# Normalisation moved behind the projections, and a later second score step, in a fused attention and mixture-of-experts kernel

## The reference

```python
xn = (x - mean(x)) / sqrt(var(x) + 1e-5)                 # over the 128 channels
# attention, 16 heads of 8 channels, causal
q, k, v = split(xn @ w_attn)
scores = q @ k.T / sqrt(8) + causal - log1p(softplus(decay_raw) * log1p(i - j))
y = softmax(scores) @ v
attn = y @ w_proj
# feed-forward, 8 experts of 128 -> 512 -> 128, each token takes the best 2
logits = xn @ Wr.T
gate = softmax over the two largest logits
ffn = sum over the 2 experts of gate * (silu(xn @ W1.T) @ W2.T)
out = x + attn + ffn
```

## Time and profile before

| what | value |
|---|---|
| median of 3 runs | 531.16 us (529.22 to 532.96) |
| profiled execution, its own time | 531.62 us |
| its span, first to last instruction | 529.8 us |
| PE busy | 482.3 us, 91% |
| DVE, ACT, POOL busy | 68%, 63%, 64% |
| chain that ended last | 72% PE, 18% DVE, 3% POOL, 2% ACT |

### The profile page before, as it was taken

One profiled execution on the slowest core, in us unless ns is written; L12 is line 12 of the kernel. 1 busy time (PEld: TensorE's weight loads), 2 busy tenths in 40 slices (PEclk: granted clock), 3 DMA queues, 4 the chain that ended last, 5 costly groups with the idle time before them and its releaser, 6 DMA issues.

```text
span 529.8 us, 13373 instructions
## 1 busy us (share of the span) xinstructions
PE 482.3 (91%) x4316; PEld 351.6 (66%) x4316; DVE 360.5 (68%) x1406; ACT 335.6 (63%) x600; POOL 338.4 (64%) x566
## 2 busy tenths in 40 slices
PE   7767999989999999999999999999999999999920
PEld 6545566555565665665565565666999999999910
DVE  7595997988988878888878878872433333333326
ACT  3578878878878878878878878776232333333300
POOL 2873555556888878876878888970454555555524
PEclk9988999999999999999999999999999999999975
DMA  6566591570460451450460451355466677666449
GB/s 179 168 232 207 156 219 47 157 214 8 136 185 23 135 173 36 137 164 23 136 181 27 137 165 50 107 171 141 121 201 190 209 215 207 207 183 207 131 166 319
DMA packets 71826, 80.38 MB, mean 152 GB/s; under 512 B 8638, under 2 KB 52672, under 8 KB 71760
## 3 DMA queue, kind: packets, MB, share of 16 engines
q1 hardware_dynamic: 67440, 71.06, 45.8%
q0 software_dynamic: 4320, 8.47, 4.5%
HBM read 48.11 MB, written 31.84 MB: 151 GB/s over the span
## 4 chain that ended last, share of the span: by engine, by line
PE 72%; DVE 18%; POOL 3%; DMA 2%; ACT 2%; issue 2%; SPq 0%; DVEq 0%; ACTq 0%; POOLq 0%
PE psT L1291 22%; PE psO L1309 13%; PE ps L1336 12%; DVE scores L1121 12%; PE psT L1363 12%; PE ps L1266 7%; PE psM L1250 2%; POOL xn_all L734 2%; DVE x_all L535 2%; PE ps L1327 1%; PE psM L1320 1%; DMA probs<-picked_dram 1%; POOL rstd L727 1%; ACT probs L884 1%; DMA decay_in<-decay_raw 1%
## 5 line engine op out<-in xcount | busy, mean ns | idle before, releaser
L1121 DVE CUSTOM_DVE_ANT_0 scores<-ps,wdist 128x256 f32<-128x256 f32 (+3 forms) x512 | 218.6, 486 | 28.1 <-PE ps L1266 25.4
L765 POOL TENSOR_SCALAR scores<-scores,row_max 128x256 f32<-128x256 f32 (+2 forms) x384 | 177.5, 477 | 62.9 <-DVE row_max L1121 61.6
L884 ACT ACTIVATE probs<-psT 128x512 f32<-128x512 f32 x320 | 173.7, 594 | 54.8 <-PE psT L1291 54.4
L1291 PE MATMUL psT<-ident,scores 128*128 128x128 f32 x1280 | 177.2, 281 | 3.4 <-ACT probs L884 2.8
L1291 PEld LDWEIGHTS psT<-ident,scores 128*128 128x128 f32 x1280 | 137.6, 141 | 63.7 <-issue 37.5
L783 POOL DMA_INDIRECT picked_dram<-scores,row_ring x71 | 69.7, 982 | 80.6 <-DVE scores L1173 79.1
L893 ACT ACTIVATE scores<-ps 128x512 f32<-128x512 f32 x71 | 42.4, 597 | 95.1 <-PE ps L1336 95.1
L846 ACT ACTIVATE scores<-scores,row_max 128x512 f32<-128x512 f32 x128 | 84.8, 714 | 0.0
L1309 PE MATMUL psO<-probs,values 128*32 128x512 f32 (+3 forms) x1024 | 82.0, 438 | 0.0
L1336 PE MATMUL ps<-scores,wdist 128*128 128x128 f32 x568 | 75.3, 276 | 0.8 <-DVE scores L1161 0.8
L1363 PE MATMUL psT<-wdist,scores 128*128 x568 | 75.3, 276 | 0.6 <-ACT scores L893 0.6
(11 more groups left out here) (140 smaller groups left out, 277.4 us busy)
## 6 DMA issues: line engine op xcount, KB each, us to landing
wdist<-w1t SPq DMA_DIRECT2D x71, 256.0 KB, 3.2
k_rows<-k_dram SPq DMA_DIRECT2D x64, 96.0 KB, 2.8
q_rows<-q_dram SPq DMA_DIRECT2D x64, 96.0 KB, 2.6
row_ring<-rows_dram SPq DMA_DIRECT2D x71, 65.0 KB, 3.0
probs<-picked_dram SPq DMA_DIRECT2D x8, 512.0 KB, 6.8
rows_dram<-row_ring SPq DMA_DIRECT2D x7, 585.0 KB, 5.8
k_dram<-k_parts SPq DMA_DIRECT2D x7, 384.0 KB, 2.3
q_dram<-q_parts SPq DMA_DIRECT2D x7, 384.0 KB, 2.6
```

The costliest lines, as they stand in the source:

```text
L765: last = nc.gpsimd.tensor_scalar(part, part, -1.0, row_max[:, r, tile, quad:quad + 1], ALU.mult, ALU.add)
L884: nc.scalar.activation(probs[:, at.ring(2), w, :], psT[:, w % 2], ACT.Exp, scale=-1.0).then_inc(exp_ready, 1)
L1121: last = nc.vector.tensor_tensor_reduce(out=scores[:, r, u, col:col + n], in0=bank[:, col:col + n], in1=wdist[:, at.g * QUADS + quad, SEQ ...
L1291: last = nc.tensor.transpose(psT[:, w % 2, place * P:(place + 1) * P], scores[:, at.ring(2), u, col + key * P:col + (key + 1) * P], ident[:])
```

## The change

Four things change.

1. Rows of batches 1 to 7 are turned raw. The weights are centred instead: PE multiplies `w_qkv` (the router's weights are now its last 8 columns) by `centre` = identity - 1/128 (step WC), and ACT copies the result back over `w_qkv`; that takes the mean off. The factor 1/std comes later: on the keys and queries by a scaling of `xt` on DVE (XN) with factors that PE turns (RT), ACT copies, SP stores (RO) and loads back spread over the partitions (RB); on the values in step V, which becomes four activations with a factor per token; on the logits in LC, which becomes a multiplication on POOL. The normalised rows that the experts need are made by POOL in slots 3 to 8 (NR, five tiles a slot).
2. The order around the start: all XB and six of the eight VL stand ahead of slot 0, in banks of their own; 12 of the 16 LN now lie in slots 0, 1 and 2 (LN 8 to 11 in slot 1 and LN 12 to 15 in slot 2, between exponentials); POOL writes the second part of the queries (QP) and takes all ten units of the maximum's subtraction in slots 0 to 2, where ACT takes none.
3. P1(1) stands behind PV 0 and 1 from slot 1 on, on every engine.
4. The sends start one slot later (slot 9).

```diff
-FIRST_SEND_SLOT = 8
+FIRST_SEND_SLOT = 9
-EARLY = {0: (("VL", 12), ("LN", 4), ("LN", 5)),
...
+EARLY = {0: {1: (("VL", 24), ("LN", 4), ("LN", 5)),
+             2: (("VL", 28), ("LN", 6), ("LN", 7)) + tuple(("LC", b * GROUPS) for b in range(6)),
+             3: (("RT", 1), ("V0", 0), ("XN", 4), ("LC", 24), ("LC", 28), ("CZ", 1)),
+             4: tuple((kind, b * GROUPS) for kind, b in (("VS", 4), ("VS", 5), ("XS", 3), ("VS", 6), ("VS", 7), ("XS", 4))
+                      ) + (("RO", 1), ("XS", 20), ("XS", 24), ("XS", 28))},
+         1: {2: (("LN", 8), ("LN", 9)), 3: (("LN", 10), ("LN", 11), ("CZ", 2))},
+         2: {2: (("LN", 12), ("LN", 13)), 3: (("LN", 14), ("LN", 15), ("CZ", 3))}}
+FIRST_ROWS_SLOT, ROW_TILES = 3, 5
...
+GROUPS_BY_POOL = 3
...
+def act_units(c):
+
+    return ACT_UNITS if c >= GROUPS_BY_POOL else ()
...
+    per_batch("XT", -4)
+    per_batch("RB", -4)
     p1(0)
-    p1(1)
+    if n == 0:
+        p1(1)
     step("TE", n - 1, NGROUP, 0, 2)
...
     step("PV", n - 2, NGROUP, 0)
     step("PV", n - 2, NGROUP, 1)
+    if n > 0:
+        p1(1)
     per_batch("KR", -3)
...
     p1(4)
+    per_batch("XN", -4)
     step("TE", n - 1, NGROUP, 8, 10)
...
+    first = TILES + ROW_TILES * (n - FIRST_ROWS_SLOT)
+    if TILES <= first < NTILE:
+        steps.append(("NR", 0, first, min(NTILE, first + ROW_TILES)))
...
 PROLOGUE = [
...
+    ("BN", 0, 0, 0, 4), ("RS", 0, 0), ("WU", 10), ("WC", 0), ("WU", 6), ("NX", 0), ("XB", 0), ("XB", 4), ("KA", 0), ("QA", 0),
+    ("BN", 0, 1, 4, 16), ("RS", 0, 1),
+    ("KR", 0), ("QR", 0), ("KM", 0), ("QM", 0), ("KL", 0), ("QL", 0), ("XB", 8), ("VL", 0),
+    ("KW", 0, 0), ("QW", 0, 0), ("KD", 0), ("QD", 0), ("QP", 0),
+    ("XB", 12), ("VL", 4), ("RT", 0), ("LN", 0), ("LN", 1), ("BN", 0, 2, 16, 20),
+    ("XB", 16), ("VL", 8), ("LN", 2), ("LN", 3), ("CZ", 0), ("BN", 0, 2, 20, 24),
+    ("XB", 20), ("VL", 12), ("BN", 0, 2, 24, 28),
+    ("XB", 24), ("VL", 16), ("BN", 0, 2, 28, 32), ("RS", 0, 2),
+    ("XB", 28), ("VL", 20),
+    ("RO", 0), ("KW", 0, 1), ("RB", 4), ("VS", 4), ("VS", 8), ("XS", 8), ("VS", 12)]
...
+                    nc.gpsimd.tensor_tensor(dst, v_stage(b)[:, :, C:], scale.broadcast_to([P, TILES, EXPERTS]), ALU.mult
+                                            ).then_inc(logits_ready, 1)
...
+                def scale_tokens(at):
...
+                    v.tensor_tensor(xt[:, at.parity, :], xt[:, at.parity, :], yt[:], ALU.mult).then_inc(xt_scaled, 1)
...
+                def centre_weights(at):
+
+                    pe.wait_ge(centre_ready, 1)
+                    pe.wait_ge(w_loaded, 16)
+                    mm(ps1[:, 0, 0:3 * C + EXPERTS], centre, w_qkv[:], start=True, stop=True).then_inc(centred_full, 1)
...
                     step = at.c * UNITS // 2 + i
+                    if step == 0:
+                        pe.wait_ge(vo_free, 5)
+                        pe.wait_ge(vm_free, 5)
```

More of the change, by code:

```diff
@@ L110 @@
 ACT_UNITS = (0, 1, 6, 7)
-POOL_UNITS = tuple(u for u in range(UNITS) if u not in ACT_UNITS)
+GROUPS_BY_POOL = 3
 FILLS = 8
@@ L124, in score_place, with pool_units, units_done @@
     return 2 * i + strip, {3: 0, 2: 0, 0: 384, 1: pair * 256}[tile]
+def act_units(c):
+    return ACT_UNITS if c >= GROUPS_BY_POOL else ()
+def pool_units(c):
+    return tuple(u for u in range(UNITS) if u not in act_units(c))
+def units_done(units, c, ready):
+    return sum(len(units(k)) for k in range(c)) + sum(u < ready for u in units(c))
 def probs_place(tile, quad):
@@ L157, in p1 @@
         route(i)
[L158 to L161, removed]
+        steps.extend((kind, c - n) for kind, c in EARLY.get(n, {}).get(i, ()))
     if n == NGROUP + 1:
@@ L174, in slot_steps @@
     per_batch("YT", 6)
-    step("SA", n, NGROUP, (0, 1))
+    if n >= GROUPS_BY_POOL:
+        step("SA", n, NGROUP, (0, 1))
     step("PV", n - 2, NGROUP, 0)
     step("PV", n - 2, NGROUP, 1)
+    if n > 0:
+        p1(1)
     per_batch("KR", -3)
@@ L442, in build @@
         xn_ready = sem("xn_ready")
-        xn_pool = sem("xn_pool")
+        rows_normal = sem("rows_normal")
+        centre_ready = sem("centre_ready")
+        centred_full = sem("centred_full")
+        centred_copied = sem("centred_copied")
+        vl_full = sem("vl_full")
+        vm_free = sem("vm_free")
+        rstd_turned = sem("rstd_turned")
+        rstd_copied = sem("rstd_copied")
+        rstd_stored = sem("rstd_stored")
+        scales_loaded = sem("scales_loaded")
+        xt_scaled = sem("xt_scaled")
         misc_full = sem("misc_full")
@@ L541, in part_rows, with write_queries @@
             return dst[at.parity].rearrange("(r k) s -> r k s", k=KINDS)[some]
+        def write_queries(engine, eng, at, part, written):
+            eng.wait_ge(misc_free, at.misc("QA", 1))
+            some = head_rows(at, part)
+            rows = part_rows(q_dram, at, some)
+            for part_no, (first, n) in enumerate(((0, 3), (3, 2), (5, 1))):
+                engine.dma_start(rows[:, first:first + n],
+                                 q_parts[some, part_no:part_no + 1].broadcast_to([some.stop - some.start, n, SEQ])
+                                 ).then_inc(written, 16)
         def head_rows(at, first):
@@ L604, in queries_write @@
                 def queries_write(at, part=1):
[L605 to L611, removed]
+                    write_queries(sp, sp, at, part, q_written if part else q_first)
                 def rows_load(dst, src, at, loaded):
@@ L728, in rstd_step, with rows_step @@
                                             ).then_inc(rstd_ready, 1)
-                def normalise_step(at):
-                    b = at.c // GROUPS
-                    pool.wait_ge(rstd_ready, 2)
-                    for t in range(b * TILES, (b + 1) * TILES):
-                        last = nc.gpsimd.tensor_scalar(xn_all[:, t, 3:], x_all[:, t, :], mean[:, t:t + 1],
-                                                       rstd[:, t:t + 1], ALU.subtract, ALU.mult)
-                    last.then_inc(xn_pool, 1)
+                def rows_step(at, first, end):
+                    for t in range(first, end):
+                        nc.gpsimd.tensor_scalar(xn_all[:, t, 3:], x_all[:, t, :], mean[:, t:t + 1], rstd[:, t:t + 1],
+                                                ALU.subtract, ALU.mult).then_inc(rows_normal, 1)
                 def logits_step(at):
@@ L868, in v_step @@
                     act.wait_ge(v_loaded, at.batches(16))
+                    act.wait_ge(rstd_ready, 3)
                     act.wait_ge(pv_full, at.groups(1, -GROUPS))
-                    nc.scalar.activation(value_cols[:, at.parity, :, :, 0:HD],
-                                         v_back[:, :, 0:C].rearrange("p t (h d) -> p t h d", d=HD),
-                                         ACT.Copy).then_inc(values_ready, 1)
+                    for t in range(TILES):
+                        tile = at.batches(TILES, t)
+                        last = nc.scalar.activation(value_cols[:, at.parity, t, :, 0:HD],
+                                                    v_back[:, t, 0:C].rearrange("p (h d) -> p h d", d=HD),
+                                                    ACT.Copy, scale=rstd[:, tile:tile + 1])
+                    last.then_inc(values_ready, 1)
                 def exp_step(at, w0, w1):
@@ L882, in exp_step @@
                     for w in range(w0, w1):
+                        if at.c == 1 and w == UNITS - 1:
+                            act.wait_ge(wdist_ready, HEADS)
                         act.wait_ge(turned, at.groups(UNITS, w + 1))
@@ L1258, in p1_step @@
                     step = at.c * UNITS // 2 + i
+                    if step == 0:
+                        pe.wait_ge(vo_free, 5)
+                        pe.wait_ge(vm_free, 5)
+                    if step == 1:
+                        pe.wait_ge(vm_free, 6)
+                        pe.wait_ge(misc_free, MISC["QA", 0] + 1)
                     if step >= 2:
```

184 lines of the change are left out of this document (126 added, 58 removed), and 12 rows, old and new, of tables (EARLY, PROLOGUE).

## The result

The changed kernel takes **544.73 us** (median; 543.43 to 546.5), the kernel before 530.84 beside it: ratio 1.0276, 95% interval 1.0247 to 1.0305. That is 13.9 us slower. Forecast were 536 us and a range of 526 to 543: the direction was right, the size was not. The profiled run took 544.62 us with a span of 542.8, 13.0 over the span before.

| | before | after | lost there | forecast |
|---|---|---|---|---|
| TE(0,2) of slot 3 starts | 65.37 | 70.11 | 4.7 | 0.3 |
| TE(0,2) of slot 9 starts | 128.36 | 134.15 | 1.1 | 0.3 |
| TE(8,10) of slot 31 starts | 355.48 | 366.18 | 4.9 | 3.7 |
| PE takes the first expert rows | 365.23 | 377.16 | 1.2 | 1.0 |
| span ends | 529.8 | 542.8 | 1.1 | 0 |

The account below looks back on a forecast made before the run. PE's list was taken to bound settled slots, and chains between engines the start. Settled slots 3.7, start 0.3, slots 3 to 8 0.3 and tail 1.0 sum to +5.3 on the median of 531.16: 536 us, range 526 to 543.

Parts of the forecast that it names:

- the start's term: Up to slot 3: TE(0,2) of slot 3 comes at 65.7 against 65.37, +0.3 us.
- the last six exponentials and the transposes that they pace: Slots 1 and 2, after each burst of logarithms: about 3.2 us until the next P1(0).
- POOL's cut: Slot 0: POOL's causal cut, 0.63 us long, ends at 36.9; DVE cannot begin slot 1 before it.
- The settled slots: Slots 9 to 31: the wait returns at P1(3), +0.26 a slot without PJ, -0.12 with, +3.7 us in all.
- the gain of 0.45 in front of TE(0,2): Each settled slot: TE(0,2) follows P1(0) after 0.37 us instead of 0.82.
- Rival B: Settled slots: P1(3) does not wait, -2.8 in place of +3.7, 530 us; chance 0.13.
- Slots 3 to 8: Slots where DVE also picks experts: +0.3 us, bounds -1.5 to +2.
- POOL's row normalisation: Slots 3 to 8: NR takes 3.9 us a slot beside 5.6 for units and fits into 10.2.
- The tail: End of slot 31: later sends delay SP's loads, so PE waits for the first expert rows, +1.0 us.
- Rival A: Start: runs at POOL's pace with ACT's bursts covered by waits, -10 there, 526 us; chance 0.17.
- Rival C: Start: Ln and Exp share a table set, so it ends 5.1 us earlier, 531 us; chance 0.07.
- Rival D: Slots with KA, QA and OT: DVE becomes the bound, +7 us, 543 us; chance 0.13.

Follow-up runs that it names:

- Experiment 10: Changed kernel with 20 unused identity matmuls on PE in each of the two pauses, in slots 1 and 2: 539.60 us.
- Experiment 4: Kernel before with only P1(1) moved behind PV 0 and 1 from slot 1 on: 535.07 us.
- the fifth kernel: Changed kernel with LN 4 to 15 all ahead of the first exponential and P1(1) directly behind TE(0,2): 525.05 us.
- experiment 11: The fifth kernel without normalisation of the expert rows, its POOL instructions cut to one column each: 525.01 us.
- experiment 3: Changed kernel with P1(1) back directly behind P1(0) and LN 4 to 15 all ahead of the first exponential: 529.40 us.
- experiment 6: The fifth kernel with the sends begun in slot 8 again instead of slot 9: 525.98 us.
- the second: Changed kernel with LN 4 to 15 all ahead of the first exponential, P1(1) left where the change put it: 530.44 us.

## Why the prediction was right or wrong

**The step that failed is the start's term, +0.3 against +4.7**, and in it the price of "the last six exponentials and the transposes that they pace", 3.2 us for each burst. They took 5.06 and 4.56. I had read the 3.2 from a settled slot, where PE never pauses and its granted clock is 1.00, and set it behind a pause of some 5 us that my own chain had just made. The kernel before had the sign in its own start, in a row that I did not use: sixteen turns behind a wait of 1.02 took 3.69 us, 0.23 each, at a granted clock of 0.54 from 48.50 to 52.20.

```profile
48.54 3.69 PE L1291 MATMUL psT<-ident,scores 128*128 128x128 f32 x16 [1.02 <-ACT probs L884]
```

Experiment 10 settles it: with PE kept busy through the pause, and the loads and logarithms where they were, the two restarts take 3.20 and 3.19. The mechanism was right, two bursts of load, Ln, load in series with the exponentials; its size was short by the restart, 1.86 + 1.36 = 3.2 of the 4.4 us missed in this term. Of the rest, 0.8 stands in slot 1 ahead of KM, where the turns and KA ran at half clock behind the wait for `q_rows` (1.97 and 1.88), though POOL's cut came 0.75 earlier than I had it (36.15, not 36.9). The rest, about 0.3, is spread over QM and the loads.

**The settled slots: the mechanism and its place right, +4.9 against +3.7.** The slots without PJ lost 0.27 (0.26 forecast). With PJ I expected -0.12 and it is -0.02: 5 x 0.10 = 0.5 of the 1.2 missing. Another 0.45 is a slip of counting: slots 3 to 31 are 29, and my sum has the gain of 0.45 in front of TE(0,2) thirty times, once in the start's term, 6 times in slots 3 to 8 and 23 times here. Experiment 4 gives the step alone +4.2. Rival B, a P1(3) that doesn't wait, is refuted by the row at 180.43.

**Slots 3 to 8: +1.1 against +0.3**, within the bounds given, but I had put POOL's row normalisation at nothing because it fits into POOL's time. It does, and still cost 1.1 us in slots 4 to 8 of the fifth kernel (experiment 11), where most of the difference stands in PE's waits for DVE, some of whose small operations take longer. That this is also why the old place of the step is so poor in these slots of the changed kernel (experiment 3) is likely, but no run has that place without the normalisation.

**The tail: +1.2 against +1.0**; experiment 6 shows it to be the one slot by which the sends start later.

**Rival A** was half right. Without the bursts the start ends at 55.78, nearly 10 us earlier, as A had it; but A's condition, bursts covered by other waits, does not hold, and I rightly gave it the smaller chance. **Rival C**: the rule of the Trainium skill (ScalarE: Activation LUTs, Table sets: the hidden batching unit), by which ln and then exp need one load, does not hold here either: between the bias's logarithms and the exponentials stand five loads of 1.28 us in the changed kernel, one in the second. **Rival D** did not come: DVE is busy for 8.40 of the 10.48 us of the settled slot shown. My range ended at the price of D and had no case in which the start's chain itself is slower by PE's clock; that case is what happened.

What the change would have been without its bursts is 530.4, no change: 8.4 us won up to P1(0) of slot 3 by raw rows, the new order and POOL's ten units, which no run tells apart, 1.3 given back in slots 3 to 8, 4.6 in slots 9 to 31 by the moved step, and 1.1 from there to the first rows; what is left of it, 1.4, no median shows. Open is why the kernel of experiment 10 gained 5.1 by its medians and only 3.9 by the profiled runs; the runs of either kernel spread by over 2 us.

## What to carry to other kernels

When a change puts a pause into PE's work, price the work behind the pause from rows that also stand behind a pause, not from the settled state: the same eight turns took 1.94 us there and 1.09 elsewhere. Keep functions that need a table load between them apart in time: eight logarithms of 5.1 us, put between exponentials, cost 14.3. Before moving a step off a wait, follow its buffer on: the 1.95 us until a pair of banks is free again made another step wait, two steps later, and the better place was one where other work lay on both sides of it.

## What the runs showed of the hardware that was not expected

- After pauses of 5.70 and 5.82 us, and after one of 3.46, PE came back at a granted clock of 0.50 to 0.57, for 3.9 to 4.8 us in the stretches read; in the kernel before it was 0.54 for 3.7 us behind a wait of 1.02. 20 matmuls without a use in each pause made the kernel 5.1 us faster by the medians, 3.9 by the profiled runs.
- Some of DVE's small operations on SBUF took two and a half to nearly six times as long beside a busy POOL: 539 ns instead of 158, 416 instead of 169, and once 2.82 us instead of 0.48. The Trainium skill (SBUF — State Buffer, SBUF: two separate sides) says that the two engines share a pair of ports as an exclusive lock, which a VectorE operation with two SBUF inputs or in a two-port mode needs, and that the loser waits for the whole instruction of the other. These rows agree that DVE waits, but in the longest case for more than one instruction: the 2.34 us that it lost cover some five of POOL's instructions of 0.48 (3.82 for 8). Three more of the same 0.48 us instructions in that run (at 67.43, 90.33 and 111.95) stand wholly beside POOL's work and took 0.48: when DVE waits and when not stays open.
- Twenty matmuls of 128x128 on the identity took 4.73 us at a granted clock of 1.00, 0.24 each and two records each (x40 in the row), where a turn of the same shape by the same identity takes 1.09 / 8 = 0.14 and one record.
